# Queries and keys of two experts and two token halves from seven block products instead of eight

## The reference

```python
rw = _gating(hidden_states, sim_matrix, gates).reshape(b, t, E)
q = jnp.einsum('btc,ech,bte->bth', hidden_states, q_proj, rw)
k = jnp.einsum('btc,ech,bte->bth', hidden_states, k_proj, rw)
v = jnp.einsum('btc,ech,bte->bth', hidden_states, v_proj, rw)
...
attn = jax.nn.softmax(scores, axis=-1)
ao = jnp.einsum('bqk,bkh->bqh', attn, v)
out = jnp.einsum('bth,ehc,bte->btc', ao, o_proj, rw)
```

## Time and profile before

| | |
|---|---|
| median of 3 runs | 3118.76 us (3117.68 to 3125.38) |
| profiled execution, its own time | 3116.84 us |
| its span, first to last instruction | 3115.3 us |
| busy in the span | PE 84%, DVE 66%, ACT 43%, POOL 13% |
| mean granted TensorE clock | 0.930 of 2.4 GHz |
| the changed stage | from about 734 to 1742 us of the span |

### The profile page before, as it was taken

The page is one execution under the profiler, slowest core; times in us unless marked ns, Lnnn a source line. Parts: engine busy times, 40 slices in busy tenths (PEclk is TensorE's granted clock), DMA queues, the critical chain, the costliest instruction groups (busy, mean ns, idle before and its releaser), DMA issues. The chain is left out here.

```text
span 3115.3 us, 66235 instructions
## 1 busy us (share of the span) xinstructions
PE 2616.4 (84%) x24651; PEld 1742.5 (56%) x24686; DVE 2055.4 (66%) x5077; ACT 1340.4 (43%) x2225; POOL 396.7 (13%) x558
## 2 busy tenths in 40 slices
PE   4867669995999999999999698987979776887457
PEld 3734446664656665665665466664657554666327
DVE  6789869995354545545454388897840386888784
ACT  3558868882010000001000377764534344666364
POOL 0012210000000000000000000001321341323104
PEclk9988779997999999999999799998989898989778
DMA  3110000002131122113111000001013220000001
GB/s 92 30 66 1 0 23 15 13 10 109 55 99 65 55 76 88 54 55 103 59 54 55 19 13 15 13 2 32 27 33 100 83 69 6 0 0 0 8 0 54
DMA packets 55136, 128.71 MB, mean 41 GB/s; under 512 B 9669, under 2 KB 21317, under 8 KB 53962
## 3 DMA queue, kind: packets, MB, share of 16 engines
q1 hardware_dynamic: 47466, 106.36, 10.4%
q0 software_dynamic: 7520, 20.34, 2.2%
HBM read 109.37 MB, written 17.30 MB: 41 GB/s over the span
## 5 line engine op out<-in xcount | busy, mean ns | idle before, releaser
L1435 PE MATMUL banks<-l1f_xe,l1f_w 128*128 128x512 f32 x1024 | 486.2, 597 | 7.9 <-DVE l1f_xe L1630 7.9
L1630 DVE TENSOR_TENSOR l1f_xe<-l1f_hT,l1f_rwb 128x512 f32<-128x512 f32 x256 | 173.4, 692 | 315.9 <-PE banks L1437 307.9
L1437 PEld LDWEIGHTS banks<-l1f_w,l1f_xe 128*128 128x128 f32 x2048 | 269.2, 192 | 123.2 <-issue 123.2
L1437 PE MATMUL banks<-l1f_w,l1f_xe 128*128 128x128 f32 x2048 | 269.8, 275 | 0.0
L1435 PEld LDWEIGHTS banks<-l1f_xe,l1f_w 128*128 128x128 f32 x1024 | 177.0, 192 | 138.4 <-issue 130.2
L1636 DVE TENSOR_TENSOR l1f_ae<-l1f_aoT,l1f_rwb 128x512 f32<-128x512 f32 x256 | 161.5, 685 | 128.6 <-PE banks L1465 128.6
L1465 PE MATMUL banks<-l1f_ae,l1f_w 128*128 128x512 f32 x512 | 233.9, 596 | 7.1 <-DVE l1f_ae L1636 7.1
L1465 PEld LDWEIGHTS banks<-l1f_ae,l1f_w 128*128 128x128 f32 x512 | 91.2, 190 | 106.0 <-issue 66.4
L214 POOL COPY x<-xn 128x512 f32 (+1 forms) x16 | 9.8, 611 | 966.2 <-DVE xn L1660 966.2
L1517 ACT ACTIVATE l1f_gw<-l1f_gw 128x64 f32<-128x64 f32 x16 | 4.1, 256 | 272.6 <-DVE l1f_gw L1611 272.6
L1105 DVE TENSOR_REDUCE l2a_top<-banks 128x16 f32<-128x1024 f32 x64 | 78.3, 1223 | 34.6 <-PE banks L1052 33.7
(11 more groups left out here) (499 smaller groups left out, 6124.4 us busy)
## 6 DMA issues: line engine op xcount, KB each, us to landing
l1f_rwb<-l1f_shares SPq DMA_DIRECT2D x128, 512.0 KB, 4.8
l0a_ctxT<-in_ctxT SPq DMA_DIRECT2D x16, 256.0 KB, 2.6
l2f_sent<-l0f_zero SPq DMA_DIRECT2D x4, 1024.0 KB, 7.0
l1a_ctxT<-in_ctxT SPq DMA_DIRECT2D x16, 256.0 KB, 2.6
l2c_ctxT<-in_ctxT SPq DMA_DIRECT2D x16, 256.0 KB, 2.6
l2e_rows<-l2f_sent SPq DMA_DIRECT2D x16, 256.0 KB, 2.8
l2f_answers<-l2e_y POOLq DMA_DIRECT2D x16, 256.0 KB, 2.7
l3p_ctxT<-in_ctxT SPq DMA_DIRECT2D x16, 256.0 KB, 2.6
```

Source lines behind the costliest of these rows:

```text
L1435: pe.matmul(bank, w[:, n, e, :], xe[:, e % NB, :], start=(e == 0), stop=(e == E - 1))
L1437: last = pe.matmul(v_bank[:, D * j:D * j + D], xe[:, e % NB, P * j:P * j + P], w[:, 2, e, :], start=(e == 0 and j == 0), stop=(e == E - 1) ...
L1630: dve.tensor_tensor(xe[:, e % NB, :], hT[:, m, :], rwb[:, m, e, :], ALU.mult).then_inc(s.xe_ready, 1)
```

## The change

Take two experts e1, e2 and the two halves (256 tokens) of a group. With the weighted inputs x(e, half), [q; k] is a 2x2 block matrix of weights times a 2x2 block matrix of inputs, eight block products. The change forms it from seven (a Strassen-Winograd form), with sums of weight blocks (`mixes`, made once by DVE in `mix` and by ACT in `minus`) and sums of inputs (`sums`, made by DVE for every pair of experts in `first_sums`, `second_sum`, `third_sum`). The seven products stay in seven halves of four PSUM banks over the eight pairs and are joined to q and k once a group (`join`). v keeps eight products of 128 columns a pair; where the first half's input is held negated, v takes the negated weights `wv_minus`.

To make room and to free DVE, more moves: attention of a group is done one step later, between the qkv pairs; `turn_rw` comes in the out phase; the normalisation is done by ACT; centring and row sum of the softmax go into ACT's exp, its scaling to ACT; `turn_y` uses the attention bank; `xe` and `ae` share one ring of eight (`feed`); `new_x` reads x itself, so that POOL makes no `xb`; the even experts' q and k weights are loaded into the second buffer of `rwb`, until the mixes are made.

The diff, cut (copies to other names, semaphore lists and shapes are left out):

```diff
+    PAIRS = E // 2
+    HT = GT // 2
+    RING_S = 2
+    NB = 8
...
+        prods = k.banks[:, 4:8, :].rearrange("p b (s n) -> p (b s) n", n=HT)
+        M2, M6, M5, M7, M3, M4, M1 = range(7)
+        W1_MINUS, T1, T2, T3_MINUS, T4_MINUS = range(5)
...
+                if isinstance(g, int) and g == 1:
+                    sp.wait_ge(s.mixes_ready, 1)
+                    sp.wait_ge(s.wv_minus_ready, 1)
...
             def turn_rw(g):
                 pe.wait_ge(s.rw_ready, g + 1)
-                wait(pe, s.rwT_ready, g)
-                pe.transpose(rw_bank[:, 0:P], rw[:, :, :].rearrange("p t e -> p (t e)"), k.ident).then_inc(s.rwT_psum, 1)
-
-            def qkv(g, e):
-                pe.wait_ge(s.xe_ready, E * g + e + 1)
-                if e == 0:
-                    pe.wait_ge(s.weights, 16 * 4)
-                    wait(pe, s.q_copied, g)
+                pe.transpose(h_bank[:, 0:P], rw[:, :, :].rearrange("p t e -> p (t e)"), k.ident).then_inc(s.rwT_psum, 1)
+
+            def product(n, left, right, p, first=False):
+
+                return pe.matmul(prods[:, n, :], left, right, start=(p == 0 and first), stop=(p == PAIRS - 1), skip_group_check=True)
+
+            def qkv(g, p):
+                at, sm = 2 * p % NB, p % RING_S
+                e1, e2 = 2 * p, 2 * p + 1
+                pe.wait_ge(s.parts_ready, 2 * (PAIRS * g + p + 1))
+                if p == 0:
+                    pe.wait_ge(s.weights, 16 * 2)
+                    pe.wait_ge(s.mixes_ready, 1)
+                    pe.wait_ge(s.wv_minus_ready, 1)
+                    wait(pe, s.q_joined, g)
                     wait(pe, s.v_copied, g)
-                for n, bank in enumerate((q_bank, k_bank)):
-                    pe.matmul(bank, w[:, n, e, :], xe[:, e % NB, :], start=(e == 0), stop=(e == E - 1))
-                for j in range(TG):
-                    last = pe.matmul(v_bank[:, D * j:D * j + D], xe[:, e % NB, P * j:P * j + P], w[:, 2, e, :],
-                                     start=(e == 0 and j == 0), stop=(e == E - 1), skip_group_check=True)
-                last.then_inc(s.qkv_psum, 1)
+                product(M1, mixes[:, W1_MINUS, p, :], feed[:, at, 0:HT], p, True)
+                product(M4, mixes[:, T4_MINUS, p, :], feed[:, at, HT:GT], p, True)
+                for j in range(TG):
+                    first, c = j < TG // 2, P * j
+                    pe.matmul(v_bank[:, D * j:D * j + D], feed[:, at, c:c + P], wv_minus[:, p, :] if first else w[:, 0, e2, :],
+                              start=(p == 0 and j == 0), stop=False, skip_group_check=True)
+                for j in range(TG):
+                    first, c = j < TG // 2, (P * j + HT) % GT
+                    pe.matmul(v_bank[:, D * j:D * j + D], feed[:, at + 1, c:c + P], w[:, 0, e2 if first else e1, :],
+                              start=False, stop=(p == PAIRS - 1), skip_group_check=True)
+                product(M2, wq[:, p, :], feed[:, at + 1, HT:GT], p, True)
+                pe.wait_ge(s.first_ready, PAIRS * g + p + 1)
+                product(M7, mixes[:, T3_MINUS, p, :], sums[:, sm, 0, :], p, True)
+                product(M5, mixes[:, T1, p, :], sums[:, sm, 1, :], p)
+                pe.wait_ge(s.second_ready, PAIRS * g + p + 1)
+                product(M6, mixes[:, T2, p, :], sums[:, sm, 2, :], p)
+                pe.wait_ge(s.sums_ready, PAIRS * g + p + 1)
+                product(M3, wk[:, p, :], sums[:, sm, 3, :], p).then_inc(s.qkv_psum, 1)
...
             def score(g):
-                pe.wait_ge(s.q_copied, g + 1)
+                pe.wait_ge(s.q_joined, g + 1)
                 wait(pe, s.ao_ready, g)
+                wait(pe, s.xn_ready, g - 1)
...
+                pe.wait_ge(s.ao_ready, upto(g + 2, k.NG))
+                four_transposes(pe, k, att_bank, yT).then_inc(s.yt_psum, 1)
...
+                for p in range(PAIRS):
+                    if p == 1 and live(2):
+                        score(n - 2)
+                    if p == 1 and live(0):
+                        turn(n)
+                    if p == 2 and live(0):
+                        logits(n, m(0))
+                    if p == 5 and live(2):
+                        turn_p(n - 2)
+                    if p == 6 and live(2):
+                        weigh(n - 2)
+                    if live(1):
+                        qkv(n - 1, p)
                 for e in range(E):
+                    if e == 1 and live(0):
+                        turn_rw(n)
+                    if e == 3 and live(3):
                         turn_y(n - 3)
...
+            def norm(g):
+                wait(act, s.hT_psum, g)
+                for j in range(TG):
+                    t = TG * g + j
+                    last = act.activation(h[:, j, :], k.x[:, bass.ds(t, 1), :].rearrange("p a c -> p (a c)"), ACT.Identity,
+                                          bias=lift[:, bass.ds(t, 1)], scale=k.rstd[:, bass.ds(t, 1)])
+                last.then_inc(s.h_ready, 1)
...
+                act.copy(hT[:, m, GT:GT + HT], h_bank[:, 0:HT])
+                act.copy(hT[:, m, HT:GT], h_bank[:, HT:GT])
+                act.activation(hT[:, m, 0:HT], h_bank[:, 0:HT], ACT.Copy, scale=-1.0).then_inc(s.hT_ready, 1)
...
+                act.copy(qk[:, 1, :], prods[:, M1, :]).then_inc(s.ends_copied, 1)
...
+                for j in range(TG):
+                    last = act.activation(prob[:, j, :], att_bank[:, P * j:P * j + P], ACT.Exp, bias=c1[:, 1, j:j + 1],
+                                          scale=float(D) ** -0.5, accum_out=c1[:, 2, j:j + 1])
+                last.then_inc(s.exp_ready, 1)
+
+            def scale(g):
+                act.wait_ge(s.rec_ready, g + 1)
+                for j in range(TG):
+                    last = act.activation(prob[:, j, :], prob[:, j, :], ACT.Copy, scale=c1[:, 3, j:j + 1])
+                last.then_inc(s.p_ready, 1)
...
+                if live(0):
+                    norm(n)
+                if live(2):
+                    exp(n - 2)
                 if live(0):
                     copy_hT(n, m(0))
+                if live(2):
+                    scale(n - 2)
+                    copy_pT(n - 2)
+                    copy_ao(n - 2, m(2))
+                if live(0):
                     gate_exp(n)
+                if live(1):
+                    copy_ends(n - 1)
+                    copy_v(n - 1)
...
+            def own_parts(g, m, p):
+
+                at = 2 * p % NB
+                dve.wait_ge(rwb_loaded[p], 16 * (g + 1))
+                if p == 0:
                     dve.wait_ge(s.hT_ready, g + 1)
-                wait(dve, s.qkv_psum, E * g + e - NB + 1)
-                dve.tensor_tensor(xe[:, e % NB, :], hT[:, m, :], rwb[:, m, e, :], ALU.mult).then_inc(s.xe_ready, 1)
+                if 2 * p < NB:
+                    wait(dve, s.y_psum, E * (g - 2) + E - NB + 2 * p + 2)
+                else:
+                    wait(dve, s.qkv_psum, PAIRS * g + p - NB // 2 + 1)
+                two = lambda ap: ap.rearrange("p (s n) -> p s n", n=HT)
+                halves = rwb[:, m, 2 * p:2 * p + 2, :].rearrange("p e (s n) -> p (e s) n", n=HT)
+                dve.tensor_tensor(two(feed[:, at, :]), two(hT[:, m, 0:GT]), halves[:, 0:4:3, :], ALU.mult).then_inc(s.parts_ready, 1)
+
+            def cross_parts(g, m, p):
+                at = 2 * p % NB
+                halves = rwb[:, m, 2 * p:2 * p + 2, :].rearrange("p e (s n) -> p (e s) n", n=HT)
+                two = lambda ap: ap.rearrange("p (s n) -> p s n", n=HT)
+                dve.tensor_tensor(two(feed[:, at + 1, :]), two(hT[:, m, HT:GT + HT]), halves[:, 1:3, :], ALU.mult)\
+                    .then_inc(s.parts_ready, 1)
+
+            def first_sums(g, p):
+
+                at, sm = 2 * p % NB, p % RING_S
+                dve.wait_ge(s.parts_ready, 2 * (PAIRS * g + p + 1))
+                wait(dve, s.qkv_psum, PAIRS * g + p - RING_S + 1)
+                two = lambda ap: ap.rearrange("p (s n) -> p s n", n=HT)
+                dve.tensor_tensor(sums[:, sm, 0:2, :], two(feed[:, at, :]), two(feed[:, at + 1, :])[:, 0:1, :].to_broadcast([P, 2, HT]),
+                                  ALU.add).then_inc(s.first_ready, 1)
+
+            def second_sum(g, p):
+                at, sm = 2 * p % NB, p % RING_S
+                dve.wait_ge(s.first_ready, PAIRS * g + p + 1)
+                dve.tensor_tensor(sums[:, sm, 2, :], sums[:, sm, 1, :], feed[:, at, 0:HT], ALU.add).then_inc(s.second_ready, 1)
+
+            def third_sum(g, p):
+                at, sm = 2 * p % NB, p % RING_S
+                dve.wait_ge(s.second_ready, PAIRS * g + p + 1)
+                dve.tensor_tensor(sums[:, sm, 3, :], feed[:, at + 1, HT:GT], sums[:, sm, 2, :], ALU.subtract).then_inc(s.sums_ready, 1)
+
+            def join(g):
+
+                dve.wait_ge(s.ends_copied, g + 1)
+                wait(dve, s.pT_psum, g)
+                two = lambda ap: ap.rearrange("p (s a) n -> p s (a n)", s=2)
```

(63 more changed lines are left out.)

146 lines of the change are left out of this document (67 added, 79 removed).

## The result

The kernel after takes 3071.38 us (median of 4 runs, 3070.32 to 3072.19), against 3122.07 us for the kernel before on the same chip (4 runs): ratio 0.985, 95% interval 0.9833 to 0.9866. The forecast was 3071, range 3060 to 3092. The profiled execution took 3070.32 us, span 3068.8.

The account below looks back on a forecast made before the run. PE's issue time was taken to bound the stage. -53.8 - 4.4 + 1.5 + 9.0 = -47.7 us from the profiled 3116.84 gave 3069.1; with 1.9 for the median of runs, 3071 us, range 3060 to 3092.

Parts of the forecast that it names:

- Products: q and k on PE: seven 256-column products take a pair from 5.22 to 4.80 us, -53.8 us in all.
- The old stall and the order: Out phase: PE's old waits of 0.29 us a step go as attention leaves it, -4.4 us.
- DVE hidden: DVE's added sums stay hidden behind PE, 45.5 of 56.8 us a step; thinnest cover 0.7 us, at `ae` 10.
- Shares hidden: Transfers of the shares, with `turn_rw` in the out phase: cost nothing, by 3.4 us of cover for PE.
- Start: Stage start: norms on ACT and hT in three copies +0.8, two DVE ops before PE +0.7: +1.5 us.
- The gap ahead of qkv(1): Between qkv(0) and qkv(1): 9.7 us against 10.1 before, taken as 0.
- End: From out(14) through out(15): longer chain +7.1, `turn_y` 0.45, slower clock +1.5, together +9.0 us.
- bare chain: Group 15's attention alone between out(14) and out(15): 11.2 us in place of 4.1, +7.1, with exp at 1.8.
- rival 1: DVE late behind join and new_x: PE waits about 1 us a step, 3086 us; chance 0.10.
- rival 2: Waits inside a pair keep PE's next weight load from starting early: 42 us, 3113, no change; chance 0.05.
- rival 3: Shares become the bound: chunk 0 over 3.4 us late makes PE wait every step, 3136 at 12.5 us landing; chance 0.04.
- rival 4: Weight loads show on PE, 0.112 us on each product instruction: +147 us, 3272; chance 0.02.

Follow-up runs that it names:

- experiment 2: Kernel after with the seven 256-column products of a pair replaced by four of 512 columns, all else in place: 3133.91 us, 1.0052 of before.
- Experiment 1: Kernel before with each 512-column q and k product issued as two 256-column halves, doubling the weight loads: 3120.49 us, 1.0006 of before.
- experiment 7: Kernel after with four more 512-wide DVE operations in front of join, once a step: 3093.32 us, ratio 0.9906.
- experiment 5: Kernel after with two more 512-wide DVE operations a pair ahead of the first sum: 3077.32 us.
- experiment 6: Kernel after with four more 512-wide DVE operations a pair ahead of the first sum: 3134.99 us (one run).
- experiment 3: Kernel after without DVE's four sums and PE's three waits for them in mid-pair; products read halves of feed: 3068.08 us, 0.9842 of before.
- experiment 11: Kernel after with PE's turn_rw eight outs later, so the shares leave 6.9 us later: 3142.89 us (one run).
- experiment 8: Kernel after with the stage's loop unrolled by four steps in place of two: 3069.97 us (one run).
- experiment 9: Kernel after with turn_rw one pair and two outs earlier, and ACT's copy of rwT ahead of its q, k, v copies: 3062.53 us, 0.9829 of before.
- experiment 12: Kernel of Experiment 10 with the stage's loop unrolled by four steps: 3060.73 us, 0.9807 of before.
- Experiment 10: Kernel of experiment 9 with the last group's attention, score through scaling, moved into the out phase before it: 3050.81 us, 0.979 of before.

## Why the prediction was right, step by step

- **Products: right.** -53.8 forecast; 4.80 us a pair in the trace, and by experiment 2 3.29 us a step, -52.6 over 16 groups. The price came from the earlier trace rows, another stage with the same shape. Experiment 1 gives an instruction a further 0.0025 us, too little to matter.
- **The old stall and the order: mis-sized.** -4.4 forecast. Before's stalls in the earlier trace rows are gone; the new order is worth 0.54 a step by experiment 2, about -8. Where the 0.25 beyond the stall comes from, the experiments do not tell apart.
- **DVE hidden: right.** "Nothing waits, but 0.7 us is the thinnest cover": 1.0 by experiment 7, and a pair had room for two more 512-wide operations but not for four (5, 6). The sums and the waits in mid-pair cost nothing in a step (3). DVE's work was put too high, 45.5 us a step and 690 in the stage, against 40.0 and 655 measured.
- **Shares hidden: right in the mean, with a gap.** "Cost nothing, by 3.4 us of cover for PE": 4.0 by experiment 11. Not forecast: the 3.9 us of four long steps. Shown: they stand behind the loop's back edge and move with it (8). In the kernel after it is DVE that pauses there, 2.4 to 3.6 us, with the first shares already landed, and PE pays what exceeds 2.1. The pause is nearly gone when the shares leave sooner (9) and gone when DVE has less to do (3); with more to do it costs more (5). With a four-step loop PE itself is 4.3 us late as well, whenever the shares leave, and the slow clock behind makes it 6 to 7 (8, 12). Instruction fetch is a likely reading of an engine that waits for nothing named, but it was not measured by itself, and how it and the transfers meet in the two-step loop stays open. A late first broadcast is not the cause: ahead of the long steps it leaves 3.6 to 3.8 us after the first store in the kernel after, but 3.3 in experiments 5, 6 and 7, which have the long steps too.
- **Start: +1.5 forecast, +1.05 measured** (first DMA to first product, 26.24 against 25.19). The gap ahead of qkv(1): 9.7 forecast, 9.4 measured, 10.1 before, so -0.7 in place of 0.
- **End: +9.0 forecast, +9.4 measured, of other parts.** The bare chain was shorter than put (pause +6.0, not +7.1; exp and its sums 1.5 us, not 1.8), out(15) behind it dearer (+3.4, not +1.95, with `turn_y`). Other traces of the same out(15) have +1.8 to +2.4, about the forecast (experiments 2, 3 and 5 to 8), or +3.1 and +3.3 (9 and 11), so this term moves with the clock. That the two errors cancel here is luck. Experiment 10 takes the 6 us of pause away.

The terms as measured: -52.6 - 8.1 + 3.9 + 1.05 - 0.7 + 9.4 = -47.1, against -45.3 in the stage; 1.8 us are not placed. The forecast's -47.7 was close since the two it missed, 3.7 us more of gain from the order and 3.9 of loss at the back edge, cancel; that is luck too. Its own range of 3062 to 3084 is 2 us low at both ends: the bounds were put around the profiled 3069.1 and not around the 3071 that was forecast, which left the stated 3060 to 3092 untouched. Rivals 1 to 4 did not happen; 2 and 4 were refuted by experiments 3 and 1, and rivals 1 and 3 were shown to begin at 1.0 and 4.0 us.

## What to carry to other kernels

Where PE is the bound and its loads hide, price a change of products by columns, with a row of the same width from any stage, and then spend the care on what runs once: the start, the gap after the first group, the bare tail. Here the gap and the tail, with the long steps that went along, gave another 16.4 us of the stage, 3050.8 in place of 3071.4 in all (experiment 10), by starting a transfer one pair sooner and putting the last group's attention beside the work of the group before. When a mean agrees with a forecast, look at the single steps: here a gain and a loss of 4 us each hid in it. And a longer unrolled loop is not free: its one back edge cost more than four of the short ones.
